# Second pass of an attention kernel issued by pairs of units, one in each 64-row tile of TensorE

## The reference

```python
# attention: 16 heads of 8 channels
qkv = (layernorm(x) @ W_qkv.T + b_qkv).reshape(bs, n, 3, 16, 8)
q, k, v = qkv[:, :, 0], qkv[:, :, 1], qkv[:, :, 2]
logits = einsum('bthc,bshc->bhts', q, k) * 8 ** -0.5
attn = softmax(where(causal, logits, -inf), axis=-1)
x = x + einsum('bhts,bshc->bthc', attn, v).reshape(bs, n, 128) @ W_proj.T + b_proj
# mixture: 8 experts of 512, the best 2 of each token
z = layernorm(x)
top_vals, top_idx = top_k(z @ Wg, 2)
# comb: softmax(top_vals) at top_idx, times alpha
x = x + sum_e (gelu(layernorm_e(z) @ fc1_w[e] + fc1_b[e]) @ fc2_w[e] + fc2_b[e]) * comb[:, e]
```

## Time and profile before

| | us |
|---|---|
| median of 3 runs | 556.99 |
| lowest and highest | 554.35, 557.75 |
| profiled execution, its time | 553.86 |
| its span, first to last instruction | 551.8 |
| TensorE busy | 484.6 |
| VectorE busy | 350.7 |
| ScalarE busy | 319.7 |
| GpSimd busy | 256.5 |

### The profile page before, as it was taken

One profiled execution on the slowest core, in us unless ns is written; L12 is line 12 of the kernel. 1 busy time (PEld: TensorE's weight loads), 2 busy tenths in 40 slices (PEclk: granted clock), 3 DMA queues, 4 the chain that ended last, 5 costly groups with the idle time before them and its releaser, 6 DMA issues.

```text
span 551.8 us, 13646 instructions
## 1 busy us (share of the span) xinstructions
PE 484.6 (88%) x4736; PEld 306.0 (55%) x4736; DVE 350.7 (64%) x900; ACT 319.7 (58%) x693; POOL 256.5 (46%) x371
## 2 busy tenths in 40 slices
PE   3278999999899999999999999888999999999920
PEld 1134445445455545545544555444888888888920
DVE  3386857778868968977877887864355722222326
ACT  2126677667667656667666766666555546465610
POOL 5755132243644445454454362352766774445520
PEclk9679999999999999999999999998999999999985
DMA  2514124133225134233314230226884697666539
GB/s 67 131 35 118 43 83 116 64 92 111 94 64 148 54 85 137 72 94 113 96 63 118 72 97 27 77 70 198 248 303 154 212 317 206 212 191 194 157 138 325
DMA packets 54068, 71.67 MB, mean 130 GB/s; under 512 B 11889, under 2 KB 39704, under 8 KB 54000
## 3 DMA queue, kind: packets, MB, share of 16 engines
q1 hardware_dynamic: 48336, 59.48, 36.4%
q0 software_dynamic: 4512, 8.70, 4.8%
q10 hardware_dynamic: 1152, 2.62, 1.4%
HBM read 36.49 MB, written 20.94 MB: 104 GB/s over the span
## 4 chain that ended last, share of the span: by engine, by line
PE 64%; DVE 24%; DMA 4%; issue 3%; POOL 2%; ACT 1%; SPq 1%; POOLq 0%; DVEq 0%; ACTq 0%
DVE row_max L976 11%; PE scores L783 11%; PE acc_bank L720 11%; PE acc_bank L792 10%; PE banks L702 7%; PE banks L706 6%; PE scores L682 4%; PE scores L687 4%; PE banks L651 3%; DMA y_in<-y_dram 2%; PE banks L638 2%; DVE xn L931 2%; PE banks L735 2%; PE banks L800 1%; PE banks L747 1%
## 5 line engine op out<-in xcount | busy, mean ns | idle before, releaser
L976 DVE TENSOR_REDUCE row_max<-scores 128x2 f32<-128x1024 f32 (+2 forms) x192 | 197.3, 1041 | 67.4 <-PE scores L687 63.0
L849 ACT ACTIVATE probs<-banks 128x512 f32<-128x512 f32 (+2 forms) x384 | 183.1, 531 | 89.9 <-PE banks L706 89.3
L706 PE MATMUL banks<-stack_q,stack_k 64*128 64x256 bf16 (+3 forms) x512 | 107.3, 296 | 0.0
L702 PE MATMUL banks<-causal_back,select 64*128 64x128 bf16 (+1 forms) x768 | 100.4, 237 | 5.6 <-DVE max_rows L982 3.1
L879 ACT ACTIVATE hidden<-scores,w_in 128x256 f32<-128x256 f32 (+1 forms) x156 | 62.9, 455 | 61.2 <-PE scores L783 61.0
L720 PE MATMUL acc_bank<-probs,v 128*32 128x512 f32 (+3 forms) x1024 | 95.3, 445 | 0.5 <-issue 0.4
L1321 POOL DMA_INDIRECT y_dram<-y,z_in x71 | 69.7, 982 | 53.0 <-DVE y L1160 36.2
L1282 POOL DMA_INDIRECT z_dram<-z,pos x64 | 62.9, 983 | 45.4 <-DVE pos L1068 27.3
L682 PE MATMUL scores<-causal,select 64*128 64x128 bf16 (+1 forms) x768 | 70.4, 241 | 14.6 <-DMA stack_k<-parts 8.2
L687 PE MATMUL scores<-stack_k,stack_q 64*128 64x256 bf16 (+3 forms) x512 | 75.4, 302 | 0.0
L702 PEld LDWEIGHTS banks<-causal_back,select 64*128 64x128 bf16 x768 | 49.1, 94 | 45.3 <-ACT probs L849 18.9
(11 more groups left out here) (172 smaller groups left out, 508.2 us busy)
## 6 DMA issues: line engine op xcount, KB each, us to landing
w_in<-in_wpack SPq DMA_DIRECT2D x39, 516.0 KB, 3.9
o_dram<-oT SPq DMA_DIRECT2D x32, 256.0 KB, 2.4
stack_k<-parts SPq DMA_DIRECT2D x47, 128.0 KB, 2.4
stack_q<-parts SPq DMA_DIRECT2D x45, 128.0 KB
z_in<-z_dram SPq DMA_DIRECT2D x32, 132.0 KB, 3.8
xt<-in_x SPq DMA_DIRECT2D x8, 256.0 KB, 3.4
onT<-o_dram SPq DMA_DIRECT2D x8, 256.0 KB, 3.4
o_inv<-inv_dram SPq DMA_DIRECT2D x8, 256.0 KB, 3.5
```

What stands on the lines that cost most here:

```text
L702: pe.matmul(cols[:, :, 0:P], select[rows(t), step, :], causal_back[rows(t), step, 0:len(heads), :], start=step == 0, stop=False, skip_grou ...
L706: mm = pe.matmul(cols[:, i, :], k[rows(t), at_head, blk * P:blk * P + P], q[rows(t), at_head, blk * P:T], start=False, stop=True, skip_gro ...
L849: act.activation(probs_of(n), columns(n), ACT.Exp, scale=SCALE).then_inc(s_exp, 1)
L976: dve.tensor_reduce(largest, used, AX.X, ALU.max).then_inc(s_max, 1)
```

## The change

The two units of a pair are put into the schedule in one tick and issued by one call on TensorE, which first waits for both banks, then alternates the matmuls between the tiles: mask, mask, mask, mask, then the scores. One increment of `s_pass2` at the end of the pair takes the place of one for each unit, so both exponentials wait for the whole pair, and the counts that others wait for are halved. `LAG` is 27, so a pair stands in the odd tick where its second unit stood before; `pv` and `pv_out` come one tick later.

```diff
-LAG = 26
+LAG = 27
...
-        if 0 <= n - LAG < G * UNITS:
-            add(("pass2", n - LAG))
+        if 0 <= n - LAG < G * UNITS and (n - LAG) % HALVES == 0:
+            add(*(("pass2", n - LAG + t) for t in range(HALVES)))
...
-                    sp.wait_ge(s_pass2, (b - STACKS + 1) * NG * UNITS)
+                    sp.wait_ge(s_pass2, (b - STACKS + 1) * NG * UNITS // HALVES)
...
-                    sp.wait_ge(s_pass2, (B - 1) * NG * UNITS)
+                    sp.wait_ge(s_pass2, (B - 1) * NG * UNITS // HALVES)
...
             def pass2(n):
-                g, u, w, heads = unit_of(n)
+                if n % HALVES > 0:
+                    return
+                g, u, w, _ = unit_of(n)
                 b, hg = divmod(g, NG)
-                wait_bank(pe, ("pass2", n))
+                for t in range(HALVES):
+                    wait_bank(pe, ("pass2", n + t))
                 if u == 0:
                     pe.wait_ge(s_mrow[g % 2], 16 * (g // 2 + 1))
-                cols = columns(n)
+                cols = [columns(n + t) for t in range(HALVES)]
+                heads = [UNIT[u + t][1] for t in range(HALVES)]
...
-                t = place(g, heads[0])[0]
                 for step in range(2):
-                    pe.matmul(cols[:, :, 0:P], select[rows(t), step, :], causal_back[rows(t), step, 0:len(heads), :],
-                              start=step == 0, stop=False, skip_group_check=True)
-                for i, h in enumerate(heads):
-                    at_head = place(g, h)[1]
-                    mm = pe.matmul(cols[:, i, :], k[rows(t), at_head, blk * P:blk * P + P], q[rows(t), at_head, blk * P:T],
-                                   start=False, stop=True, skip_group_check=True)
+                    for t in range(HALVES):
+                        pe.matmul(cols[t][:, :, 0:P], select[rows(t), step, :], causal_back[rows(t), step, 0:len(heads[t]), :],
+                                  start=step == 0, stop=False, skip_group_check=True)
+                for i in range(len(heads[0])):
+                    for t in range(HALVES):
+                        at_head = place(g, heads[t][i])[1]
+                        mm = pe.matmul(cols[t][:, i, :], k[rows(t), at_head, blk * P:blk * P + P], q[rows(t), at_head, blk * P:T],
+                                       start=False, stop=True, skip_group_check=True)
                 mm.then_inc(s_pass2, 1)
...
-                wait(act, s_pass2, n + 1)
+                wait(act, s_pass2, n // HALVES + 1)
```

## The result

Medians of 20 runs each: 558.26 us after, 554.57 before, ratio 1.0058 with a 95% interval of 1.0041 to 1.0075. The change makes the kernel slower by 0.6%, some 3.2 us by the ratio (the medians lie 3.7 apart). The forecast was 553.0, that is 4 us under the 557.0 of the three runs it started from; the median of 20 is 554.57, so that start lay 2.4 us too high. The result lies in the range (537 to 565) and in "within 1%", but the sign is wrong: against the change by -4 us stands one of +3.2, and the near miss of the figure 553.0 says little. A second measurement of the same kernel (after_same_chip, beside the experiments of the third set) gave 557.94 against 554.89, ratio 1.0067 [1.004, 1.0093].

A forecast was written before the change was run, and what follows sets the result against it. TensorE, busy 88% of the span, was taken as the bound, with the three-bank ring limiting at MAXT. Splits -10.5 and exposed MAXT legs +7.0 gave -3.5, or -5 counted singly; -4 us was taken: 553.0 us, range 537 to 565.

The forecast's parts named there:

- within 1%: Outcome from 551.4 to 562.6 us, not told from no change: chance 45%.
- part (1): 25 splits between 512-column units (PROJ, K, ZT, GATE): pairing saves 0.42 us each, 10.5 us, if ScalarE is not late.
- part (2): 31 splits by MAXT: the saved unit is not paid out, and a plain leg costs 0.41 us more.
- 0.06 to TensorE: Hand-over from the end of a ScalarE exponential to TensorE's next matmul, taken as 0.06 us.
- from U8 to the next U2+3: Rest of a plain group: same order but for V and P changed over, counted as no cost.
- The tail: Stretch without first pass, from 358 us: GATE -0.8, PROJ -0.4, V0 waiting twice for the copy +0.8, together -0.4 us.
- MAXT leg: Stretch from U2+3 to U8 around MAXT: 0.41 us longer in a plain group, hidden by VectorE waits in front groups.
- Adjacent pairs mix by themselves: TensorE already runs 124 of 192 pairs side by side; only the 68 split by a fill can save array time.
- the in-order rival: Matmuls issue strictly in program order, so 124 pairs gain 0.31 us more each, 38 us: 515 us; chance 2%.
- U5 waits already: Behind MAXT, U5 starts exactly when U3's exponential ends, so the ring of three banks is the limit there.
- full gain (530.5): Rival: TensorE paces and each of the 68 splits pays, 26.5 us, giving 530.5 us; chance 20%.
- The rival with the ring: MAXT's pair and V0 wait behind ScalarE's L854 copy: +9.4 us, 566.4; decides once a group loses 0.33; chance 19%.

The follow-up runs named there:

- third set: Experiments run on one chip beside the kernel before, whose median there was 554.9 us.
- one_wait: Changed kernel, but pairs whose banks were both last used by second-pass units wait once, other pairs twice with the younger bank first: 555.64 us, ratio 1.0005.
- single_same_chip: Repeat of single_units in the third set: ratio 0.992 to the kernel before.
- copy_placed: copy_between, but in the rank group the accumulator copy stays behind the exponential of U5: 548.34 us, ratio 0.9871 to the kernel before.
- single_units: Changed kernel's schedule, but each unit issued by itself with its own bank, wait and increment: 550.33 us, ratio 0.9918 to the kernel before.
- joint_wait: single_units, but the first unit of a pair waits for both banks: 591.19 us on the slower chip, ratio 1.0013 to the kernel before.
- after_again: The changed kernel once more, unaltered, on the slower chip of the second set: one single run, 592.15 us.
- copy_sooner: Changed kernel with ScalarE's accumulator copy and the output's store one tick earlier: 559.99 us, ratio 1.0091 to the kernel before.
- between_same_chip: Repeat of copy_between in the third set: 549.02 us, ratio 0.9876 to the kernel before.
- second set: Experiments run on a slower chip beside the kernel before, whose median there was 591.6 us.
- copy_between: single_units with ScalarE's accumulator copy between the exponentials of U4 and U5: ratio 0.9812 to the kernel before, on the slower chip.

## Why the prediction was wrong, and where it was right

An account by sections of the span. The windows of the kernel before: to the first P3, the first batch, the five batches with the front groups, the rest:

```profile
0.00:54.87 54.87, 29.39 (x258) 14.33 (x259) 30.79 (x55) 17.90 (x32) 32.62 (x66) 0.84 0.37 88
54.87:102.53 47.66, 45.55 (x586) 23.52 (x583) 34.88 (x58) 33.86 (x74) 10.98 (x26) 1.00 0.26 77
102.53:323.66 221.13, 212.41 (x2486) 112.88 (x2482) 177.85 (x444) 148.04 (x311) 102.55 (x157) 1.00 0.32 93
323.66:551.80 228.14, 197.22 (x1421) 155.29 (x1417) 107.22 (x346) 119.94 (x279) 110.32 (x122) 0.95 0.59 187
```

The same sections of after_same_chip:

```profile
0.00:57.63 57.63, 32.20 (x250) 15.21 (x252) 30.93 (x55) 17.63 (x31) 32.70 (x66) 0.76 0.34 84
57.63:107.11 49.48, 42.45 (x583) 20.71 (x580) 34.07 (x55) 34.31 (x74) 11.00 (x26) 1.00 0.25 74
107.11:326.41 219.30, 189.06 (x2483) 97.47 (x2483) 179.87 (x448) 146.84 (x310) 102.71 (x157) 1.00 0.33 94
326.41:556.40 229.99, 192.44 (x1427) 151.57 (x1423) 107.05 (x346) 120.49 (x280) 110.76 (x122) 0.95 0.59 185
```

And its third section in one_wait, with one front group of 14.92 instead of 13.36 in it:

```profile
103.90:322.27 218.37, 190.57 (x2483) 94.72 (x2483) 179.92 (x448) 147.15 (x310) 102.66 (x157) 0.99 0.33 94
```

| section | forecast | after_same_chip less before |
|---|---|---|
| to the first P3 | 0 | +2.8 (clock 0.76 against 0.84) |
| first batch and the rest together | +0.5 | +1.8 and +1.9 |
| five batches | -4.1 | -1.8 |

The forecast's column is its own sum, sorted: a batch has -1.68 + 0.42 + 0.5 and some -0.05, -0.8, times five; what is left of the -3.5 is +0.5.

- **The step that failed is the hand-over in the working of part (1), used again in part (2): "0.06 to TensorE".** It measured 0.14, since the wait that comes last stands in an instruction of its own. Three pairs of a plain group wait for ScalarE (U4+5, U6+7, U10+11), and two of them are on the path; what follows U6+7 waits for the copy, which stands behind U5's exponential. That makes the plain group +0.70 instead of +0.41 and the rank one +0.78 instead of +0.5. One_wait takes 0.08 off the plain leg and 0.10 off the rest of the group. In it the five batches take 216.8 without its dip, 4.3 less than before, where the forecast had 4.1. The hand-over is 2.9 of the 7.2 us between the forecast's -4 and the +3.2.
- **A second term stood at nothing without a reason that held**: "from U8 to the next U2+3 ... I count that as nothing ... U11 waits for U8's exponential before as after". Before, U10 went ahead at its own bank (58.98, U11 at 59.50); in a pair U10 waits too. That is the 0.12 above, 0.02 with one_wait. In the late group the leg was to be hidden, -0.1 to 0; it cost 0.17 in four of five batches, because the forecast read the late group of the first steady batch (8.99), the only one that takes longer than 8.80 before. The rank groups account for 1.4 us of what the five batches missed and the late ones for 0.9.
- **The tail was the third.** The step was "V0 waits for the copy twice (+0.8)" less GATE and PROJ, -0.4 in all. From the fourth section's start to the last RANK on the PE timeline the kernel before takes 57.7 us (323.66 to 381.34), after_same_chip 59.4 (326.41 to 385.80), single_same_chip 58.2 (318.78 to 376.96) and copy_placed 56.8 (322.14 to 378.95). So, by one execution each, the order of TensorE alone gains 0.9 there, the copy behind both exponentials takes 1.4 (single_same_chip against copy_placed) and the joint claim 1.2 more. I had the copy at 0.8 and the claim at nothing: +1.7 instead of -0.4. What is behind the last RANK takes 170.5 before and 170.6 after: the feed-forward stage was moved as a whole, as said.
- **The first batch** lost +1.8: its four legs like the plain one are each 0.4 to 0.7 longer, and its second group is 0.66 shorter. I had spread its splits and its legs over the kernel and not taken it singly. With one_wait it is 48.92, still 1.3 longer, so the hand-over is about a third of it.
- **The front group**: forecast 13.4 to 13.6, measured 13.45, so the MAXT leg is hidden there. **The gate group**: forecast 10.8, measured 10.95, 10.86 with one wait.
- **Adjacent pairs mix by themselves**: right. Single_units is slower than the kernel with alternated tiles in one group of the steady batches only (the first late one, 9.11 against 8.96), and the in-order rival, with 38 us of gain, is out. The Trainium skill (TensorE: Matmul & The Clock Gate, "The mechanism") lets matmuls start strictly in program order; this case's runs differ, since U3's masks start beside U2's and ahead of U2's score (316.68 and 316.80 above).
- **U5 waits already, so the ring is the limit at MAXT**: right, and the reason that the full gain (530.5) did not come. What I did not see is that the order of claims had a cheap way out. Single units in the new order let U4 go at its own bank: a plain group costs 0.1 to 0.2 (8.36 to 8.48 against 8.24), and a batch of single_same_chip is 1.3 shorter (221.13 less 216.25 less its dip of 1.57, over five), where the four splits were to give 1.68. *The rival with the ring* (slower, 566.4) named the right place, V0 behind L854 and the pair's banks. A batch of after_same_chip is 0.37 shorter than before (1.83 over five), so its four groups lost 1.68 - 0.37 = 1.31, or 0.33 each: just the point from which that rival decides, where I took 0.22. Its other condition came in part: the front groups hide the leg, the late ones all but 0.17.

The four sections sum to +4.6, the medians of the same set to +3.1. The 2.8 of the first section depend on the clock. Kernels of the new order whose clock stayed at 1.00 there reach the first P3 at 54.8 to 55.0 (one_wait, single_same_chip, copy_placed, joint_wait), and so does after_again (55.0). The kernel before is there at 54.87 with a shorter dip (0.66 from 27.3 to 37.6). But after, after_same_chip and copy_sooner get there at 56.9, 57.6 and 57.3, each with the same dip to 0.50, and no other kernel has it. So a part of the +3.1 may be a dip that the change brings about in most executions, beside the +1.8 of the other sections. That is not shown: three profiles have it and one, on another chip, has not.

## What to carry to other kernels

Before units in different 64-row tiles are paired by hand, look whether the trace shows them mixed already; if so, the pairing is worth only what its *order* saves, and that can be had by moving the fills, without one unit's start hanging on the other's bank. A joint claim of two buffers in a ring of three gives up a part of the ring. Of two waits ahead of a matmul on the critical path, the one that ends last must not be the separate one, which here was the one written second: where both are on one counter, wait once for the larger count; where they are not, write first the one that ends last, as one_wait does for U6+7. And after a unit is moved, read what stands on the other engine between the two exponentials that now come in a burst: the place of one copy of 0.6 us was worth 0.44% between the ratios here (0.992 and 0.9876, whose intervals just overlap) and 0.15 us in each plain group.

## What was not expected of the hardware

- **A separate wait that is released last costs some 0.09 us.** Hand-over from ScalarE's last exponential to TensorE's first matmul: 0.14 when the wait for it is an instruction of its own, 0.04 to 0.05 when the weight load carries it, even beside a second wait that is over (the chains and the lines of L410 above). A plain group has it three times, twice on the path, and one_wait takes 0.18 us off the group.
- **The clock falls in front groups, and not in all.** TensorE stands idle for the same 1.29 us ahead of XNT in both of these rows of copy_placed's PE timeline, and takes 0.63 once and 1.02 the other time:

```profile
105.63 0.63 PE L640 MATMUL banks<-ident,xn 128*128 128x128 f32 x4 [1.29 <-DVE max_rows L984]
148.54 1.02 PE L640 MATMUL banks<-ident,xn 128*128 128x128 f32 x4 [1.29 <-DVE max_rows L984]
```

  The granted clock is 1.00 in the first group and 0.66 from 148 to 153 in the second; at full speed that clock is 2.4 GHz, and its lower level is 1.2. It costs 1.57 us a time: four times in copy_placed, once each in the first profile of the kernel after, in one_wait, in single_same_chip and in between_same_chip, and not in the one profile of the kernel before, where the idle is 1.17. It is not in single_units, after_same_chip or copy_sooner either, so whether the shorter front group brings it about is not shown. Whether a few matmuls put into that wait would hold the clock wasn't tried; it would be worth up to 6 us in copy_placed.
- **Chips differ.** The same kernel before took 591.6 us in the second set and 555 in the two others, 6.6% more. The kernel after ran there with gate, rank and plain groups as on the other chip, to 0.03, but late groups of 9.6 to 9.9 instead of 8.96, and from the last RANK (397.15) to the end of its span (589.3) it took 192.2 us instead of 170.5: 21.7 us of the 32.9 between its two spans lie in the feed-forward stage. The cause is open. Ratios moved too: copy_between was 0.9812 there and 0.9876 in the third set, intervals apart.
